# Statistics of the first stage's rows, roots of the degrees, and the order of the last attention stage

## The reference, cut to what matters

```python
x = x + L0_gnn(ln(x), adj)   # two convolutions, distances exp(-d)*adj, a GRU cell
x = x + L0_ffn(ln(x))        # 16 experts, 2 for each token
x = x + L1_gnn(ln(x), adj)   # norm = (sum(adj, -1) + 1e-6) ** -0.5, two products with adj
x = x + L1_ffn(ln(x))        # 8 experts, 1 for each token, with a capacity
x = x + L2_gnn(ln(x), adj)
x = x + L2_ffn(ln(x))        # slice attention and a scan
x = x + L3_gnn(ln(x), adj)   # attention, 8 heads, log adj as bias
x = x + L3_ffn(ln(x))        # rms norm, causal attention with 4 heads, rms norm, 8 experts, 2 for each token
```

## Time and profile before

| | us |
|---|---|
| median of 3 runs | 3415.86 (3410.84 to 3417.27) |
| the profiled execution | 3411.13 |
| its span | 3409.4 |
| PE / DVE / ACT / POOL busy | 2626.2 / 2287.1 / 1767.5 / 854.4 |
| mean granted clock of PE | 0.904 |

### The profile page before, as it was taken

One profiled execution on the slowest core, in us unless ns is written; L12 is line 12 of the kernel. 1 busy time (PEld: TensorE's weight loads), 2 busy tenths in 40 slices (PEclk: granted clock), 3 DMA queues, 4 the chain that ended last, 5 costly groups with the idle time before them and its releaser, 6 DMA issues. The chain is left out here.

```text
span 3409.4 us, 68862 instructions
## 1 busy us (share of the span) xinstructions
PE 2626.2 (77%) x19386; PEld 2090.6 (61%) x19386; DVE 2287.1 (67%) x6715; ACT 1767.5 (52%) x5080; POOL 854.4 (25%) x844
## 2 busy tenths in 40 slices
PE   3999965991875923689999997898885777739993
PEld 2777755991775923566777765565562544429993
DVE  5777753566674665577777775688884777725555
ACT  1334323663663634556555553666663666516664
POOL 0233343661352523200000000000001234433442
PEclk9999987995886966899999998899997999959996
DMA  5112202234321213100000000000001000012225
GB/s 184 50 56 65 65 20 65 83 86 147 101 63 46 68 57 131 47 1 1 0 0 0 0 0 11 25 19 18 25 13 57 14 20 25 24 34 60 63 62 170
DMA packets 142548, 168.55 MB, mean 49 GB/s; under 512 B 19920, under 2 KB 118224, under 8 KB 141776
## 3 DMA queue, kind: packets, MB, share of 16 engines
q1 hardware_dynamic: 117744, 120.77, 11.7%
q0 software_dynamic: 21504, 44.74, 3.7%
q10 hardware_dynamic: 3168, 1.49, 0.2%
HBM read 115.87 MB, written 51.05 MB: 49 GB/s over the span
## 5 line engine op out<-in xcount | busy, mean ns | idle before, releaser
L1145 POOL DMA_INDIRECT y_rows<-ffn_e_rows_out,ffn_e_scatter_at x352 | 340.9, 969 | 435.3 <-DVE ffn_e_rows_out L1173 251.5
L1286 PE MATMUL bank<-ffn_e_xT,ffn_e_mine 128*128 128x128 f32 x3360 | 438.1, 277 | 2.1 <-ACT ffn_e_xT L1219 1.4
L1286 PEld LDWEIGHTS bank<-ffn_e_xT,ffn_e_mine 128*128 128x128 f32 x3360 | 408.8, 194 | 3.4 <-ACT ffn_e_xT L1219 2.2
L889 POOL DMA_INDIRECT sorted_rows<-ffn_r_h,ffn_r_slot x320 | 322.0, 1006 | 314.9 <-issue 314.6
L1221 ACT ACTIVATE ffn_e_mine<-constants 128x512 f32 (+1 forms) x352 | 250.1, 712 | 125.2 <-issue 77.3
L1193 DVE TENSOR_TENSOR ffn_e_hid<-ffn_e_act,bank 128x256 f32<-128x256 f32 (+1 forms) x280 | 136.0, 486 | 224.3 <-ACT ffn_e_act L1246 186.6
L1296 PE MATMUL bank<-ffn_e_mine,ffn_e_hid 128*128 128x128 f32 x1968 | 278.1, 276 | 2.3 <-DVE ffn_e_hid L1197 1.9
L1296 PEld LDWEIGHTS bank<-ffn_e_mine,ffn_e_hid 128*128 128x128 f32 x1968 | 247.5, 192 | 5.0 <-DVE ffn_e_hid L1197 4.5
L2487 ACT ACTIVATE gnn_prob<-bank,gnn_low 128x256 f32<-128x256 f32 x512 | 193.9, 490 | 51.9 <-DVE gnn_low L2405 51.9
L2405 DVE TENSOR_REDUCE gnn_low<-bank 128x2 f32<-128x512 f32 x256 | 158.9, 683 | 63.4 <-PE bank L2581 63.3
L2593 PE MATMUL bank<-ident,gnn_prob 128*128 128x128 f32 x1024 | 145.9, 277 | 42.7 <-DVE gnn_probT L2416 32.2
(11 more groups left out here) (504 smaller groups left out, 6617.8 us busy)
## 6 DMA issues: line engine op xcount, KB each, us to landing
g_adj<-in_adjT SPq DMA_DIRECT2D x48, 512.0 KB, 3.9
ffn_e_rows_in<-sorted_rows SPq DMA_DIRECT2D x346, 66.0 KB
ffn_c_y<-y_rows SPq DMA_DIRECT2D x80, 256.0 KB, 3.3
g_adj_rows<-in_adj SPq DMA_DIRECT2D x16, 512.0 KB, 4.2
gnn_adj<-in_adjT SPq DMA_DIRECT2D x16, 512.0 KB, 3.9
constants<-in_ffn SPq DMA_DIRECT2D x1, 6281.0 KB, 18.3
y_rows<-ffn_e_rows_out,ffn_e_scatter_at POOLq DMA_INDIRECT x352, 2.2
constants<-in_ffn SPq DMA_DIRECT2D x1, 5204.0 KB, 16.1
```

What stands on the lines that cost most here:

```text
L889: g.indirect_dma_start(self.c.sorted_rows, bass.IndirectOffsetOnAxis(self.slot[par][:, k, j:j + 1], 0), self.h[par][:, j, :], None).then_i ...
L1145: g.indirect_dma_start(c.y_rows, bass.IndirectOffsetOnAxis(scatter_at[par][:, k:k + 1], 0), rows_out[par][:, k, :], None).then_inc(scatter ...
L1286: ins = pe.matmul(chunk(part, ch), chunk(weights[:, i * HALF:(i + 1) * HALF], ch), x, start=True, stop=True)
```

## The change

Seven edits. (1) SP issues only the first half of x, ACT the second, and DVE takes no statistics while loading. (2) In gnn0, DVE first prepares taps and constants, then takes the statistics of 16 tiles and their factors, and then normalises turn 0. Tiles 16 to 31 come at the end of turn 0, tiles 32 to 63 and the factors of 48 tiles at the end of turn 1. (3) The constants of ffn0 are issued behind the adjacency of turn 1, not before all of it. (4) The roots of the degrees go to POOL in `moe_combine` of ffn0. (5) att3 begins with the power and the factors of 8 columns; the power of the other 56 follows at once on POOL, and their factors come on DVE behind `rope_k(0, 0)`. (6) In att3's turns ACT copies heads 1 and 2 and DVE heads 0 and 3; `vector_first` moves from the end of a turn to the start of the next, `vector_shift` from before `rope_q` to behind `vector_second`, `scalar_rows` behind `evac_o(t - 1, 1)`. (7) Behind the last turn the routing of the last three turns is mixed with the rest of the attention.

```diff
 def begin_phase(nc, c, name, nxt):
+    begins = name == c.order[0]
-            if nxt:
+            if nxt and not begins:
                 sp.dma_start(c.block[nxt], c.dram[nxt]).then_inc(c.w_ready[nxt], 16)
-        if name not in MOE:
+        if name not in MOE and not begins:
...
+def row_factors(v, c, sems, at=slice(None)):
+    merged, var_eps, rstd = sems
+    mean_variance(v, c, merged, at)
+    v.tensor_scalar(c.var_eps[:, at], c.MV[:, at, 1], EPS, None, ALU.add).then_inc(var_eps, 1)
+    v.wait_ge(var_eps, 1)
+    rsqrt(v, c, rstd, at)
+    return v.scalar_tensor_tensor(c.shift[:, at], c.MV[:, at, 0], -1.0, c.rstd[:, at], ALU.mult, ALU.mult)
...
                     sp.dma_start(adj_rows[par][:], c.adj[t]).then_inc(adj_rows_ready[par], 16)
+                    if isinstance(t, int) and t == 1:
+                        nxt = c.order[1]
+                        sp.dma_start(c.block[nxt], c.dram[nxt]).then_inc(c.w_ready[nxt], 16)
...
                 route.pool_dispatch(g, TURNS - 2, 0)
-                g.wait_ge(degrees_done, TURNS)
-                g.tensor_scalar(c.norm[:], c.norm[:], 1e-6, None, ALU.add).then_inc(degrees_ready, 1)
-                g.wait_ge(degrees_ready, 1)
-                g.tensor_tensor(c.norm[:], c.norm[:], c.minus_half[:], ALU.pow)
                 route.pool_dispatch(g, TURNS - 1, 1)
...
+                def statistics(part):
+                    v.wait_ge(c.x_in[part], 16)
+                    with v.Fori(4 * part, 4 * part + 4) as i:
+                        for k in range(TT):
+                            tile = ds(i * TT + k, 1)
+                            ins = v.bn_stats(c.ST[:, tile, :], c.X[:, tile, :])
+                        ins.then_inc(counted_rows, 1)
+                    v.wait_ge(counted_rows, 4 * part + 4)
+                FIRST, REST = slice(0, 16), slice(16, TILES)
+                statistics(0)
+                row_factors(v, c, early, FIRST).then_inc(factors_ready, 1)
+                v.wait_ge(factors_ready, 1)
+                normalise(v, c, 0, h).then_inc(h_ready, 1)
...
                     if not first:
                         route.vector_gates(v, t - 1, before)
+                    if first:
+                        statistics(1)
+                    if second:
+                        statistics(2)
+                        statistics(3)
+                        row_factors(v, c, late, REST).then_inc(factors_ready, 1)
+                        v.wait_ge(factors_ready, 2)
...
+            if name == "ffn0":
+                @block.gpsimd
+                def _(g):
+                    g.tensor_scalar(c.norm[:], c.norm[:], 1e-6, None, ALU.add).then_inc(degrees_ready, 1)
+                    g.wait_ge(degrees_ready, 1)
+                    g.tensor_tensor(c.norm[:], c.norm[:], c.minus_half[:], ALU.pow)
...
-    ACT_T = ((0, 2), (1, 2))
+    ACT_T = ((0, 1), (0, 2), (1, 1), (1, 2))
+    EARLY = 2 * TT
...
+                for at in (slice(0, EARLY), slice(EARLY, TILES)):
+                    if at.start == 0:
+                        g.wait_ge(square_ready, 1)
+                    g.tensor_tensor(rs2[:, at], mean_sq[:, at], c.minus_half[:, at], ALU.pow).then_inc(rs2_ready, 1)
                 route.pool_begin(g)
-                g.wait_ge(square_ready, 1)
-                g.tensor_tensor(rs2[:], mean_sq[:], c.minus_half[:], ALU.pow).then_inc(rs2_ready, 1)
...
                 rope_q(0, 0)
                 rope_k(0, 0)
+                factors(1, slice(EARLY, TILES))
...
                     T(0, 0)
+                    if since(t, 3):
+                        route.vector_first(v, t - 3, 1 - par, three)
                     if since(t, 2):
                         route.vector_stats(v, t - 2, two)
                     scores_low(t, 0)
-                    T(0, 1)
-                    if since(t, 2):
-                        route.vector_shift(v, t - 2, par, two)
                     if not last:
                         rope_q(t + 1, 1 - par)
                     T(0, 3)
                     if since(t, 3):
                         route.vector_second(v, t - 3, three)
+                    if since(t, 2):
+                        route.vector_shift(v, t - 2, par, two)
...
                     scores_low(t, 1)
-                    T(1, 1)
...
                         new_rows(t - 1)
-                    if since(t, 2):
-                        route.vector_first(v, t - 2, par, two)
...
                         evac_hT(t + 1)
+                    T(0, 1)
                     exp(t, par, 0, 0)
                     exp(t, par, 0, 1)
+                    T(0, 2)
                     exp(t, par, 0, 2)
-                    T(0, 2)
                     exp(t, par, 0, 3)
                     if not first:
                         evac_o(t - 1, 0)
-                    if since(t, 2):
-                        route.scalar_rows(a, t - 2, par)
...
                         evac_o(t - 1, 1)
+                    if since(t, 2):
+                        route.scalar_rows(a, t - 2, par)
                     if not last:
                         evac_v(t + 1, 1 - par)
+                    T(1, 1)
                     exp(t, par, 1, 0)
...
+                A, B, Z = TURNS - 3, TURNS - 2, TURNS - 1
+                outputs_T(Z, True)
+                route.tensor_rank(pe, A)
+                tokens_T(Z, True)
+                route.tensor_hT(pe, B, B % 2)
+                final(Z)
+                pe.wait_ge(route.picked, B)
+                route.tensor_logits(pe, B)
+                route.tensor_rank(pe, B)
+                route.tensor_hT(pe, Z, Z % 2)
...
-                for k in range(4):
+                for k in (0, 1):
                     sp.dma_start(c.X[:, 16 * k:16 * k + 16, :], x_tiles[:, 16 * k:16 * k + 16, :]).then_inc(x_in[k], 16)
+            @block.scalar
+            def _(a):
+                for k in (2, 3):
+                    a.dma_start(c.X[:, 16 * k:16 * k + 16, :], x_tiles[:, 16 * k:16 * k + 16, :]).then_inc(x_in[k], 16)
```

More of the change, by code:

```diff
@@ L105, in begin_phase @@
 def begin_phase(nc, c, name, nxt):
-    s = {k: c.sem(f"{name}_{k}") for k in ("merged", "var_eps", "rstd")}
-    k = c.order.index(name)
+    begins = name == c.order[0]
+    sems = [c.sem(f"{name}_{k}") for k in ("merged", "var_eps", "rstd")]
     with nc.Block() as block:
@@ L2848, in turn @@
                         new_rows(t - 1)
[L2849 to L2850 removed]
                 every_turn(v, turn, begin=3)
[L2852 to L2867 removed]
+                A, B, Z = TURNS - 3, TURNS - 2, TURNS - 1
+                evac_T(Z, 1, 1, 0)
+                route.vector_first(v, A, A % 2, A + 1)
+                route.vector_second(v, A, A + 1)
+                route.vector_stats(v, B, B + 1)
+                evac_T(Z, 1, 1, 3)
+                route.vector_chosen(v, A, A + 1)
+                route.vector_shift(v, B, B % 2, B + 1)
+                norm_o(Z, 1)
+                route.vector_places(v, A, A % 2, A + 1)
+                route.vector_gates(v, A, A + 1)
+                new_rows(Z)
+                route.vector_stats(v, Z, Z + 1)
+                route.vector_first(v, B, B % 2, B + 1)
+                route.vector_second(v, B, B + 1)
+                route.vector_shift(v, Z, Z % 2, Z + 1)
+                route.vector_chosen(v, B, B + 1)
+                route.vector_places(v, B, B % 2, B + 1)
+                route.vector_gates(v, B, B + 1)
+                route.vector_first(v, Z, Z % 2, Z + 1)
+                route.vector_second(v, Z, Z + 1)
+                route.vector_chosen(v, Z, Z + 1)
+                route.vector_places(v, Z, Z % 2, Z + 1)
+                route.vector_gates(v, Z, Z + 1)
             @block.scalar
@@ L2872, in rows_h @@
                     wait_past(a, hT_ps, t)
+                    if isinstance(t, int) and t == EARLY // TT:
+                        a.wait_ge(rows_scaled, 2)
                     for k in range(TT):
@@ L2960, in _ @@
                 every_turn(a, turn, begin=3)
-                evac_T(TURNS - 1, 1, 1, 2)
-                evac_o(TURNS - 1, 0)
-                evac_o(TURNS - 1, 1)
-                evac_onT(TURNS - 1)
-                route.scalar_exp(a, TURNS - 3)
-                for t in (TURNS - 2, TURNS - 1):
-                    route.scalar_rows(a, t, t % 2)
-                    route.scalar_hT(a, t)
-                    route.scalar_exp(a, t)
+                A, B, Z = TURNS - 3, TURNS - 2, TURNS - 1
+                evac_T(Z, 1, 1, 1)
+                evac_T(Z, 1, 1, 2)
+                route.scalar_exp(a, A)
+                evac_o(Z, 0)
+                evac_o(Z, 1)
+                route.scalar_rows(a, B, B % 2)
+                evac_onT(Z)
+                route.scalar_hT(a, B)
+                route.scalar_exp(a, B)
+                route.scalar_rows(a, Z, Z % 2)
+                route.scalar_hT(a, Z)
+                route.scalar_exp(a, Z)
             @block.tensor
@@ L3170, in program @@
         c.w_ready = {n: c.sem("w_ready_" + n) for n in order}
```

(10 more changed lines are left out.)

132 lines of the change are left out of this document (55 added, 77 removed).

## The result

| | before | after |
|---|---|---|
| median of 4 runs, us | 3414.88 (3410.84 to 3417.27) | 3363.97 (3359.99 to 3367.15) |
| ratio | 1 | 0.9855, 95% interval 0.9842 to 0.9867 |
| profiled execution's span | 3409.4 | 3358.2 |

A forecast was written before the change was run, and what follows sets the result against it. No engine was held full in att3's turns; waits bound them: dispatches, landing, L773, then rope_q; DVE's order set the start. Terms 10.6 - 10.7 - 9.0 - 28.7 - 12.5 = -50.3 gave 3360.8, forecast 3363 us, range 3342 to 3390.

The forecast's parts named there:

- The first stage: Start and first turns of gnn0: earlier first L369 -11.4, statistics in the turns +17.0, clock +5, together +10.6 us.
- 5 for the clock: gnn0's first turns: PE's clock falls to 0.50 behind three new gaps, costing +5 us (0 to 6).
- Roots: End of gnn0: the power leaves POOL's stream ahead of the last dispatch, -11.2, with semaphore clears +0.5: -10.7 us.
- Start of att3: Start of att3: a power of 8 columns in 1.65 instead of 10.58 brings ACT's rows earlier, -9.0 us.
- The turns of att3: Middle of att3: later shift no longer waits, turns of 21.5 instead of 24.0; 11 turns save 27.7, with the last 28.7.
- without the wait the loop is that of the attention: att3's turns: path over ACT's evacuation, rows, copies and exponents to the last product sets the turn, 21.0 plus 0.5.
- The end: Tail of att3: last routing mixed with the attention's rest, -12.5 us; the last turn's saving of 1 was counted separately.
- a power on POOL holds up DVE: Rival, ffn0's combine and att3's start: POOL's power excludes DVE work, 15 less gain, 3377 us; chance 0.10.
- DVE and nothing else sets the turn: Rival, att3's turns: DVE alone bounds them, a turn of 20.4, total 3348 us; chance 0.18.
- The dispatch still sets the turn: Rival, att3's turns: the dispatch loop is only shifted, pitch stays 23.6 to 24, total 3389 us; chance 0.13.
- ACT was not the bound: Rival, att3's turns: ACT, given head 1's copies, becomes the bound, total 3423 us; chance 0.04.

The follow-up runs named there:

- after_again: The changed kernel, unaltered, run again beside the kernel before: 3363.99 against 3412.98 us, ratio 0.9857.
- t2_early: The changed kernel with ACT's copy of head 2 in front of att3's first exponents: 3364.53 against 3412.98 us for the kernel before, ratio 0.9857.
- stats_late: t2_early with vector_stats behind T(0, 3) and vector_shift behind rope_k: 3336.96 against 3412.98 us for the kernel before, ratio 0.9778.
- shift_early: The changed kernel with vector_shift back in front of rope_q: 3395.86 against 3412.98 us for the kernel before, ratio 0.9950.
- experiment 2: Ran att_only and old_start beside the kernel before (3604.02 and 3594.05 against 3623.83 us); also grouped new-start traces by PE's clock in turn 1.
- att_only: The kernel before with edits (5) to (7) alone, on a chip with long att3 turns: 3604.02 against 3623.83 us, ratio 0.9939.
- old_start: The changed kernel with edits (1) to (3) undone, on a chip with long att3 turns: 3594.05 against 3623.83 us for the kernel before, ratio 0.9912.

## Why the prediction was right, and where not

Forecast 3363, measured 3363.97; a sum of -50.3, and 51.2 of span in the two traces. The sum came out better than its terms, and that is luck: errors of both signs cancelled.

- **The first stage, +10.6 forecast, +7.2 measured.** The wait for ffn0's constants is there. They landed at 43.8, not at 46.0 (22.2 behind their issue at 21.6; the 2.1 MB of adjacency ahead of them are also 6.0 and not 6.3 at 350 GB/s), so L386 came at 44.2 in place of 46.2: 2.0 of the difference. The third L386 was forecast at -11.4 + 17.0 = +5.6 without the clock, and the trace has +5.3, but by two errors: the 2.0, and two distances of L386, 29.03 and 41.44, that are 1.8 longer together than the sum's 28.27 and 40.45. With the 1.8 behind the third L386, what came on top of the statistics is 3.6, where the sum has 5 for the clock: the other 1.4. This is one execution. In after_again, t2_early, stats_late and shift_early, with the same start, the dispatches in the middle of gnn0 are 9.8, 7.3, 10.8 and 9.5 later than before, by PE's clock in turn 1 as experiment 2 sorts them.
- **Roots, -10.7 forecast, -11.1 in the trace**, -9 and -12 by two runs alone. ffn0 gained 2.4 that no step spoke of; the other executions show it to be scatter.
- **Start of att3, -9.0 forecast, -9.3 measured.** ffn3's constants do hold `vector_begin` (5.15), and not `rope_q`. The power of 8 columns took 1.7 as worked out. Up to the first L2847 4.0 more went, which no step has. Of the fourteen traces, the eight with `k` 12.8 behind ACT's first rows had won them, the six with 14.6 not. The three with the old att3 are among the six, but the order of the engines' work doesn't sort the rest: att_only and old_start have the same att3, and fell on either side. In the changed kernel PE has 1.00 from 2586 to 2591; the kernel before has 0.50 from 2602 to 2607, where it does the same, and all fourteen sort in this way. So it is the clock; what decides it is open.
- **The turns of att3, -27.7 forecast for 11 turns, -21.5 measured** between the same rows (242.6 in place of 264.2), and the turn before them became 1.5 longer: -20.0 in all. The first half of the mechanism was right: the wait at the shift left (the earlier trace rows against an L797 that waits in none of the turns 3 to 14), and putting it back cost 32. The second half was not. The step "without the wait the loop is that of the attention", followed over ACT's evacuations, copies and exponents, names the wrong path: ACT's copy could be moved for nothing (t2_early), and 1.6 less of DVE's work ahead of `rope_q` and `rope_k` made the turn 1.3 shorter (stats_late). DVE's order set the turn, and that the path followed came to 21.0, beside the 21.2 of a turn at full clock, is luck. The size failed for another reason: I had no term for a clock that falls in every second turn and costs 2.0, so the mean was 22.1 and not 21.5, although show that it fell in the kernel before. There it did in five of the eleven turns, the three of 25.1 and two of 23.6.
- **The end, -13.5 with the last turn, -12.5 measured.** The last 16 dispatches follow one another as worked out.

Of the rivals, "a power on POOL holds up DVE" is refuted by the L1403 of 793.80, 0.69 inside the power, by the 26 like it in the twelve traces, and by L2797, 0.26 beside the second power of att3. This is against the rule named there from the Trainium skill (SBUF — State Buffer, Who interferes with whom) for this power and these additions. "DVE and nothing else sets the turn" named the right engine, though not its price of 20.4: stats_late shows that DVE's order up to `rope_q` and `rope_k` was worth 1.3 a turn, with DVE busy for 18.0 of 21.2. "The dispatch still sets the turn" was wrong for the changed kernel, and right again as soon as the shift goes back. ACT was not the bound: moving its copy moved nothing. Against the sum, the turns gave 8 less and the end 1 less; the first stage cost 3.4 less, and 2.4 in ffn0 and 4.0 at att3's start are in none of its terms: the errors cancelled.

## What to carry to other kernels

Before moving a wait, find the instruction behind it on which the next turn hangs, and shorten the way to that one: the wait with the largest sum (21.8 us) could be removed for nothing, and 1.6 of other work ahead of `rope_q` and `rope_k` were worth 27 us. Ask for the granted clock of single turns, not of the stage: turns that alternate in length with the same work are its sign. Work that is moved to start a stage earlier should go where its engine is idle by the trace, not to the end of a turn that is full.

## What the hardware showed that I had not expected

- One kernel, the kernel before, took 3413, 3624 and 3653 us on three chips. On the latter two ACT and DVE stood in nearly every middle turn of att3 until 2.1 to 2.9 us behind the start of the last of 8 indirect transfers, and a turn took 27 to 29 in place of 23.6. More of the difference, 73 us, lies in ffn0, and no run here asks why.
- The granted clock after a stand of PE is not the same from run to run: at the start of att3 the same instructions took 12.8 or 14.6, and the third turn of the first stage began at 114.7 or at 117.4 in the same kernel.
- DVE adds two 128x512 f32 inputs from SBUF in its usual 0.69 while a power on POOL runs for 10.58.
